# Graph layers on one core: the bias row laid by ScalarE under an adding load of x, a new order of the first graphs, and a chain per half of the last graph

## The chip, the cores and the metric

The kernel runs on one core of a Trainium2 chip. The metric is the device time of one execution in microseconds (us); lower is better. The engines are PE (TensorE), DVE (VectorE), ACT (ScalarE), POOL (GpSimd) and SP (SyncE, which here only issues DMAs). Sixteen DMA engines move data between HBM and SBUF.

## The reference, cut to what matters

There are 64 graphs of 256 nodes with 512 features. Each goes through two layers, all in fp32:

```
h  = relu(layernorm(x))
q, k, v = h @ Wq.T + bq, h @ Wk.T + bk, h @ Wv.T + bv
w  = adj * exp(q @ k.T);  w = w / sum(w, axis=2)
x1 = x + w @ v                                    # layer 0, with its residual
h1 = relu(layernorm(x1))
L  = (adj + I) scaled by d = (row sums)**-0.5 on both sides
y  = x1 + L @ (h1 @ W + b)                        # layer 1, with its residual
```

Since the rows of w sum to one, the value bias can be added behind the product: `x1 = (x + bv) + w @ (h @ Wv.T)`. The kernel keeps `x + bv` in the tile `xb`. The change is mostly about who makes `xb`.

## The kernel before

Everything is written by hand: each engine has its own program, which waits on semaphores. A product in fp32 is made of three fp32r products of rounded and rest parts (`_hi`, `_lo`), so each operand of TensorE is first split, as a rule by ACT (`_hi`) and DVE (`_lo`).

A function `steps` calls, on every engine, `step(0)`, `step(1)`, `step(2)`, a loop over 3 to 62, then `step(63)`, `step(64)` and `step(65)`. `step(k)` does the main part of graph k (flag `main`), the second layer of graph k-1 (`prev`) and the first preparations of graph k+1 (`ahead`). `step(0)` prepares weights and graph 1, `step(65)` is the second layer of the last graph alone.

On PE a steady step is, in this order: G (48 matmuls, `ps<-ht_hi,m_hi`, the weights Wq and Wk folded into m), the values V1 to V7 (42, `ps<-wt_hi,...`), Z of the graph before (24, `ps<-hat_hi,h_hi`: the normalized adjacency times h1), S (24, `ps<-ht_hi,g_hi`), O1 of the graph before (24 of 512 columns, `ps<-w_hi,z_hi`: the second layer's weight) and O (24, `ps<-v_hi,p_hi`).

`ht`, the transposed h, is made by a trip through HBM: ACT writes `h`, SP stores it (`h_scratch`), waits, loads it back in blocks of 32 by 32 with four DMAs of 128-byte rows (`h_blocks`), and DVE turns the blocks (L681, `transpose_h`). All this goes over SP's one queue. In SP's step the order is: `adj_in` (waits for `rsum_ready`, from ACT's `keep_adjacency`), the store of h, the four loads of `h_blocks`, the load of x into `xb` (L243), the load of x of two graphs on (`x_in`), the small trip of the row norms (`dn_scratch`, `dn_row`), the four `adj_blocks`, the two stores of y.

The steps that the change and the prediction touch:

- `xb`: SP loads x, POOL waits for it and adds `bv_row` (L345, two instructions a graph), after the power that makes `dn` (L334) and before its four sums `ht_sum` (L292 to L297). DVE reads `xb` when it makes x1 (L718, under the tile name `late`).
- DVE behind `h_blocks`: the two turns of `ht` (L681), `v_u`, `v`, `vk`, `v` (L642), `v<-v_u,v_p` (L644), `v_lo` (L648), `vk`, `v_lo` (L653), then `z_lo` (L785, twice), for which PE's O1 waits, then `v_lo` (L658), `p` (L798), and so on.
- The first graphs: ACT splits `w_hi` (L394) in `step(0)`; the layer norm of graph 2 is made in the middle of `step(1)`.
- The last graph: in `step(64)` PE does both halves of O1 of graph 63 and then O of graph 64; in `step(65)` DVE makes x1 and its statistics for both halves, POOL one power for both, ACT h1, DVE `h_lo`, then PE does Z and O1.

## Time and profile before

| | us |
|---|---|
| median of 3 runs | 1664.22 (1661.92 to 1664.26) |
| the profiled execution, its own time | 1666.89 |
| span of that execution, first to last instruction | 1665.1 |
| mean granted TensorE clock | 0.994 of full speed |
| PE busy | 1628.0 (98%) |
| DVE, ACT, POOL busy | 1434.1, 1071.2, 842.6 |

A row of the timeline reads: start, duration, engine, line, operation, output <- inputs, shape, count, and in brackets how long the engine had been idle before and who released it. Matmuls overlap, so the distance between two starts says what one costs. Engines with a q (SPq, ACTq) are queues of DMA issues: their duration is that of issuing, not of the transfer. All tiles that share the buffer `late` (wq, wk, x1, h1, x1b, y) are called `late`.

### The profile page before, as it was taken

The page shows a single profiled execution, that of the slowest core. Times are in us where ns is not written, and L with a number is a line of the kernel's source. Part 1 is how long each engine was busy: PE and PEld are TensorE (multiplying, and loading weights), DVE is VectorE, ACT ScalarE, POOL GpSimd, SP SyncE. Part 2 cuts the span into 40 slices and gives each one's busy share as a digit, 9 for nine tenths or more (in the row PEclk, how much of TensorE's full clock was granted, in tenths as well). Part 3 has the DMA queues.
Part 4 walks back from the last instruction along what each step waited for, and adds up shares of the span by engine and source line. Part 5 has one row for each costly group of instructions (what it writes and reads, how often), then busy time and mean ns, then how long its engine had stood idle before and what let it go on. Part 6 is the DMA issues. An engine that isn't in the chain of part 4 may idle for free.

```text
span 1665.1 us, 37788 instructions
## 1 busy us (share of the span) xinstructions
PE 1628.0 (98%) x12010; PEld 1544.7 (93%) x12010; DVE 1434.1 (86%) x3366; ACT 1071.2 (64%) x2451; POOL 842.6 (51%) x968
## 2 busy tenths in 40 slices
PE   8799999999999999999999999999999999999997
PEld 6789999999999999999999999999999999999996
DVE  6778888888889889888888888888888888888885
ACT  5656566676666666676576676676676676676552
POOL 2445555555555555555555555555555555555551
PEclk9999999999999999999999999999999999999999
DMA  5344544544544544544544544545544544544530
GB/s 171 89 127 119 145 121 125 148 121 119 153 120 120 152 120 122 152 124 124 145 125 123 148 121 119 152 122 125 148 122 122 149 126 126 143 123 122 147 98 29
DMA packets 494415, 212.66 MB, mean 128 GB/s; under 512 B 402496, under 2 KB 427072, under 8 KB 494400
## 3 DMA queue, kind: packets, MB, share of 16 engines
q1 hardware_dynamic: 492480, 210.89, 48.4%
q10 hardware_dynamic: 1920, 1.58, 0.3%
q8 instruction: 8, 0.13, 0.0%
q14 instruction: 7, 0.06, 0.0%
HBM read 146.28 MB, written 66.13 MB: 128 GB/s over the span
## 4 chain that ended last, share of the span: by engine, by line
PE 45%; DMA 14%; DVE 14%; ACT 10%; issue 9%; SPq 5%; POOL 3%; ACTq 0%; DVEq 0%; POOLq 0%
PE ps L854 15%; PE ps L856 14%; PE ps L857 14%; DMA h_blocks<-h_scratch 7%; DMA h_scratch<-h 6%; SPq L185 3%; ACT h L423 3%; DVE v L644 2%; ACT unused_x L436 2%; DVE z_lo L785 2%; DVE ht L681 1%; ACT adj_kept L445 1%; DVE v_lo L653 1%; ACT ht_hi L533 1%; ACT p_hi L524 1%
## 5 line engine op out<-in xcount | busy, mean ns | idle before, releaser
L345 POOL TENSOR_TENSOR xb<-xb,bv_row 128x512 f32<-128x512 f32 x128 | 169.0, 1341 | 432.7 <-DMA xb<-in_x_dram 394.3
L854 PE MATMUL ps<-ht_hi,m_hi 128*128 128x256 f32 x1024 | 286.2, 280 | 0.0
L856 PE MATMUL ps<-ht_lo,m_hi 128*128 128x256 f32 x1024 | 285.8, 279 | 0.0
L857 PE MATMUL ps<-ht_hi,m_lo 128*128 128x256 f32 x1024 | 285.6, 279 | 0.0
L413 ACT ACTIVATE g_hi<-ps,u_col 128x256 fp32r<-128x256 f32 x256 | 105.7, 464 | 204.9 <-PE ps L857 204.9
L854 PE MATMUL ps<-w_hi,z_hi 128*128 128x512 f32 x512 | 205.3, 401 | 11.9 <-DVE z_lo L785 11.8
L857 PE MATMUL ps<-w_hi,z_lo 128*128 128x512 f32 x512 | 203.0, 396 | 0.0
L856 PE MATMUL ps<-w_lo,z_hi 128*128 128x512 f32 x512 | 202.9, 396 | 0.0
L854 PEld LDWEIGHTS ps<-ht_hi,m_hi 128*128 128x128 f32 x1024 | 192.5, 188 | 0.0
L857 PEld LDWEIGHTS ps<-ht_hi,m_lo 128*128 128x128 f32 x1024 | 192.4, 188 | 0.0
L856 PEld LDWEIGHTS ps<-ht_lo,m_hi 128*128 128x128 f32 x1024 | 192.4, 188 | 0.0
L304 POOL TENSOR_TENSOR ht_sum_lo<-ht_sum,ht_sum_hi 128x512 fp32r<-128x512 f32 x128 | 163.5, 1299 | 13.5 <-ACT ht_sum_hi L408 11.4
L854 PE MATMUL ps<-hat_hi,h_hi 128*128 128x256 f32 x512 | 145.4, 284 | 7.7 <-DVE h_lo L747 7.7
L854 PE MATMUL ps<-wt_hi,ht_sum_hi 128*128 128x256 f32 (+1 forms) x512 | 144.9, 283 | 4.9 <-POOL ht_sum_lo L304 2.5
L854 PE MATMUL ps<-v_hi,p_hi 128*128 128x258 f32 (+1 forms) x512 | 144.6, 282 | 1.5 <-DVE ht_lo L822 0.9
L486 ACT ACTIVATE v_hi<-v 128x256 fp32r<-128x256 f32 x64 | 26.9, 421 | 184.1 <-DVE v L642 184.0
L857 PE MATMUL ps<-hat_hi,h_lo 128*128 128x256 f32 x512 | 145.2, 284 | 0.0
L856 PE MATMUL ps<-hat_lo,h_hi 128*128 128x256 f32 x512 | 145.1, 283 | 0.0
L857 PE MATMUL ps<-ht_hi,g_lo 128*128 128x256 f32 x512 | 145.1, 283 | 0.0
L856 PE MATMUL ps<-ht_lo,g_hi 128*128 128x256 f32 x512 | 144.6, 283 | 0.0
L854 PE MATMUL ps<-ht_hi,g_hi 128*128 128x256 f32 x512 | 144.6, 282 | 0.0
L856 PE MATMUL ps<-wt_lo,ht_sum_hi 128*128 128x256 f32 (+1 forms) x512 | 144.5, 282 | 0.0
(147 smaller groups left out, 5646.8 us busy)
## 6 DMA issues: line engine op xcount, KB each, us to landing
x_in<-in_x_dram SPq DMA_DIRECT2D x64, 512.0 KB, 5.0
xb<-in_x_dram SPq DMA_DIRECT2D x64, 512.0 KB, 4.4
out_dram<-late SPq DMA_DIRECT2D x128, 256.0 KB, 2.1
h_scratch<-h SPq DMA_DIRECT2D x62, 512.0 KB, 3.5
h_blocks<-h_scratch SPq DMA_DIRECT2D x248, 128.0 KB, 3.6
adj_in<-in_adj_dram SPq DMA_DIRECT2D x64, 256.0 KB, 2.9
adj_blocks<-in_adj_dram SPq DMA_DIRECT2D x256, 64.0 KB, 2.5
dn_row<-dn_scratch SPq DMA_DIRECT2D x64, 128.0 KB, 2.9
```

Of the source, the lines that this page charges most:

```text
L185: sp.dma_start(h_blocks[q * 32:(q + 1) * 32].rearrange("r c (g j) -> r c g j", j=32), rows[q]).then_inc(h_blocks_loaded, 16)
L304: pool.tensor_tensor(ht_sum_lo[:, pair], ht_sum[:, pair], ht_sum_hi[:, pair].bitcast(fp32), ALU.subtract).then_inc(ht_sum_lo_ready, 1)
L345: last = pool.tensor_tensor(xb[:, t, :], xb[:, t, :], bv_row[:], ALU.add)
L413: last = act.activation(g_hi[:, m, :], ps[:, G + j, m % 2 * N:m % 2 * N + N], ACT.Identity, bias=u_col[:, m:m + 1])
L423: act.activation(h[:, t, :], x_in[:, t, :], ACT.Relu, scale=rs_x[:, t:t + 1], bias=nb_x[:, t:t + 1]).then_inc(h_ready[t], 1)
L436: last = act.activation(unused_x[:, t, :], x_in[:, t, :], ACT.Square, bias=neg_mean[:, t:t + 1], accum_out=x_square[:, t:t + 1])
L486: act.activation(v_hi[:, 0, 1, 0:HD], v[:, 0, 1, 0:HD], ACT.Copy).then_inc(v_hi_ready[1], 1)
L644: dve.tensor_tensor(v[:, 1, 1, 0:HD], v_u3[:, 0:HD], v_p5[:], ALU.add).then_inc(v22_ready, 1)
L785: dve.tensor_tensor(z_lo[:, 2 * j:2 * j + 2, :].rearrange("p c n -> p (c n)"), ps[:, Z + j, :], z_hi[:, 2 * j:2 * j + 2, :].rearrange("p c ...
L854: pe.matmul(dst, a_hi[:, c, cols], b_hi[:, c, :], start=(first and c == 0), stop=False, skip_group_check=not first)
L856: pe.matmul(dst, a_hi[:, c, cols], b_lo[:, c, :], start=False, stop=False, skip_group_check=not first)
L857: end = pe.matmul(dst, a_lo[:, c, cols], b_hi[:, c, :], start=False, stop=(c == chunks - 1), skip_group_check=not first)
```

## The change

Three things are changed together.

1. `xb`: ACT copies `bv_row` into both halves of `xb` as soon as x1 of the graph before is made (`fill_xb`), and POOL issues a DMA that loads x and adds it to what lies in `xb` (`x_with_bias`, `accum_op=ADD`). SP's load of `xb` and POOL's two additions go.
2. The first graphs: `w_hi` is made on POOL; the adjacency of graph 1 is turned on DVE in `step(0)`; sums, squares and layer norm of graph 2 are made earlier; the transposed h of graph 2 has its own PSUM banks; `keep_p1` of step 2 comes between the halves of h1; 20 warm-up matmuls in place of 12. ACT now waits in `step(0)` for both bias rows ahead of its first sums.
3. The last graph: x1, statistics, power, scale and h1 go half by half; Z is made half by half; O1 of its second half goes in two pieces of 256 columns, each stored by itself; the second half of O1 of graph 63 comes behind O of graph 64.

In every step but the last, `v_lo` of L653 moves behind `z_lo`.

```diff
         def _(sp):
...
-            sp.dma_start(xb[:], x[0].rearrange("(t p) d -> p t d", p=P)).then_inc(xb_loaded, 16)
...
-                if main and prev:
-                    x_this = x_flat[bass.ds(sp.snap((this - 1) * (N * D)), N * D)]
-                    sp.wait_ge(x1_ready[0], this - 1)
-                    sp.wait_ge(x1_ready[1], this - 1)
-                    sp.dma_start(xb[:], x_this.rearrange("(t p d) -> p t d", p=P, d=D)).then_inc(xb_loaded, 16)
...
         def _(pool):
...
+            def x_with_bias(graph):
+                x_this = x_flat[bass.ds(pool.snap((graph - 1) * (N * D)), N * D)]
+                pool.wait_ge(xb_filled, graph)
+                pool.dma_start(xb[:], x_this.rearrange("(t p d) -> p t d", p=P, d=D),
+                               accum_op=ALU.add).then_inc(xb_ready, 16)
...
+                if main and prev:
+                    pool.wait_ge(d_ready, this - 1)
+                    pool.wait_ge(dn_turned_ready, this - 1)
+                    row_norms(this)
+                    x_with_bias(this)
                 if ahead and not main:
                     x_power(this + 1)
+                    row_norms(this + 1)
+                    x_with_bias(this + 1)
                     ht_sums(this + 1)
                     ht_sums_low(this + 1)
-                if main:
-                    if not prev:
-                        pool.wait_ge(bias_rows_loaded, 32)
-                    pool.wait_ge(xb_loaded, this * 16)
-                    for t in range(NT):
-                        last = pool.tensor_tensor(xb[:, t, :], xb[:, t, :], bv_row[:], ALU.add)
-                    last.then_inc(xb_ready, 1)
                 if main and not prev:
                     x_power(this + 1)
+                    pool.wait_ge(w_loaded, 16)
+                    pool.tensor_copy(w_hi[:], w_in[:]).then_inc(w_hi_ready, 1)
...
         def _(act):
...
+            def fill_xb():
+                for t in range(NT):
+                    last = act.activation(xb[:, t, :], bv_row[:], ACT.Copy)
+                last.then_inc(xb_filled, 1)
...
                     hat_high(this - 1)
+                if main and prev:
+                    act.wait_ge(x1_ready[0], this - 1)
+                    act.wait_ge(x1_ready[1], this - 1)
+                    fill_xb()
...
                 if ahead and not main:
+                    act.wait_ge(bias_rows_loaded, 32)
                     x_sums(this + 1)
                     x_squares(this + 1)
                     layer_norm_x(this, prev, older)
+                    fill_xb()
                     keep_adjacency(this + 1)
...
         def _(dve):
...
+                    transpose_adjacency(this + 1, False)
+                    turn_dn(this + 1, False)
                     for j in range(2):
                         dve.wait_ge(ht_done[j], this + 1)
...
         def _(pe):
...
-                for k in range(12):
+                for k in range(20):
...
+                if main and prev:
+                    first_result(0, this)
+                    if ahead:
+                        first_result(1, this)
...
+                if main and not ahead:
+                    first_result(1, this)
+                if prev and not main:
+                    last_graph(this - 1)
```

What POOL's program has in the loop, from the power that makes `dn` to its first sum of `ht`, before:

```order
L332 TENSOR_TENSOR rsum<-rsum,ones 128x2
L334 TENSOR_TENSOR dn_wide<-rsum,minus_half 128x2
L343 REGISTER_ALU
L345 TENSOR_TENSOR xb<-xb,bv_row 128x512 x2
L290 REGISTER_ALU
L292 TENSOR_TENSOR ht_sum<-ht 128x256
```

and of the change, with ACT's rows of the same stretch (from the sums of the adjacency to the scaling into h1) behind them:

```order
L288 TENSOR_TENSOR rsum<-rsum,ones 128x2
L290 TENSOR_TENSOR dn_wide<-rsum,minus_half 128x2
L295 ISA
L295 DMA xb<-in_x_dram 128x2x512
L301 REGISTER_ALU
L303 TENSOR_TENSOR ht_sum<-ht 128x256
```

```order
L450 ACTIVATE adj_kept,rsum<-adj_in 128x256 x2
L461 ACTIVATE hat_hi<-adjt 128x512
L456 ACTIVATE xb<-bv_row 128x512 x2
L418 ACTIVATE g_hi<-ps,u_col 128x256 x2
L488 ACTIVATE late<-late,nb,sc 128x512
```

The additions and their wait are gone from POOL; a DMA issue stands in their place, and ACT has two more copies between `hat_hi` and `g_hi`.

DVE's program at the start, from the shift of graph 1's layer norm to the first split of `ht`, before and then of the change:

```order
L672 TENSOR_TENSOR nb_x<-neg_mean,rs_x 128x2
L769 COPY ht<-ps 128x512 x2
L773 COPY wt<-ps 128x2x256 x2
L822 TENSOR_TENSOR ht_lo<-ps,ht_hi 128x512 x2
L570 TENSOR_TENSOR m_lo<-ps,m_hi 128x512 x4
```

```order
L697 TENSOR_TENSOR nb_x<-neg_mean,rs_x 128x2
L715 STREAM_TRANSPOSE adjt<-adj_blocks 128x512
L723 STREAM_TRANSPOSE dn_turned<-dn_wide 128x32
L848 COPY ht<-ps 128x512
L848 COPY ht<-ps 128x512
L852 COPY wt<-ps 128x2x256 x2
```

The turn of the adjacency blocks and the turn of `dn` now stand ahead of the copies of `ht`.

DVE's program for the last graph, from the last `p_lo` to the first rows of `h_lo`, before and then of the change:

```order
L842 SCALAR_TENSOR_TENSOR late<-ps,d,late 128x512 x2
L716 RECIPROCAL rinv<-ps 128x1
L718 SCALAR_TENSOR_TENSOR late<-ps,rinv,xb 128x512
L721 BN_STATS st<-late 128x6
L716 RECIPROCAL rinv<-ps 128x1
L718 SCALAR_TENSOR_TENSOR late<-ps,rinv,xb 128x512
L721 BN_STATS st<-late 128x6
L727 TENSOR_SCALAR d<-dn_wide 128x2
L729 BN_AGGR mv<-st 128x2 x2
L732 TENSOR_SCALAR ve<-mv 128x2
```

```order
L746 SCALAR_TENSOR_TENSOR late<-ps,d,late 128x512
L751 RECIPROCAL rinv<-ps 128x1
L753 SCALAR_TENSOR_TENSOR late<-ps,rinv,xb 128x512
L758 BN_STATS st<-late 128x6
L764 BN_AGGR mv<-st 128x2
L766 TENSOR_SCALAR ve<-mv 128x1
L751 RECIPROCAL rinv<-ps 128x1
L753 SCALAR_TENSOR_TENSOR late<-ps,rinv,xb 128x512
L770 TENSOR_TENSOR sc<-rs,dn_wide 128x1
L772 SCALAR_TENSOR_TENSOR nb<-mv,sc 128x1
```

The second y of graph 63 has moved behind these rows, and the scale of half 0 stands ahead of the statistics of half 1.

## Rows read from the trace of the kernel before

**Rows 1.** Waits of PE: who for whom, us in total, times, longest.

```profile
PE ps L854 <- DVE z_lo L785: 11.8, 15, 3.0
...
PE ps L854 <- ACT v_p L398: 3.2, 1, 3.2
...
PE ps L854 <- DVE v_u L627: 1.8, 1, 1.8
PE ps L889 <- ACT h L423: 1.7, 1, 1.7
```

**Rows 2.** Timeline: DVE's z_lo of one step, PE's first O1 of four steps.

```profile
75.20 1.27 DVE L785 TENSOR_TENSOR z_lo<-ps,z_hi 128x512 fp32r<-128x512 f32 x2
...
76.73 0.47 PE L854 MATMUL ps<-w_hi,z_hi 128*128 128x512 f32 x1 [0.60 <-DVE z_lo L785]
...
833.75 0.40 PE L854 MATMUL ps<-w_hi,z_hi 128*128 128x512 f32 x1
...
858.58 0.40 PE L854 MATMUL ps<-w_hi,z_hi 128*128 128x512 f32 x1
...
1633.57 0.40 PE L854 MATMUL ps<-w_hi,z_hi 128*128 128x512 f32 x1
```

**Rows 3.** Timeline of DVE in one step of the loop, from the turn of ht.

```profile
827.15 1.30 DVE L681 STREAM_TRANSPOSE ht<-h_blocks 128x512 f32<-128x512 f32 x2 [0.29 <-DMA h_blocks<-h_scratch]
...
829.67 1.46 DVE L644 TENSOR_TENSOR v<-v_u,v_p 128x256 f32<-128x256 f32 x1
...
831.51 0.50 DVE L653 TENSOR_TENSOR v_lo<-v,v_hi 128x256 fp32r<-128x256 f32 x1
831.94 1.27 DVE L785 TENSOR_TENSOR z_lo<-ps,z_hi 128x512 fp32r<-128x512 f32 x2
```

**Rows 4.** Timeline of POOL in the same step.

```profile
821.16 0.69 POOL L334 TENSOR_TENSOR dn_wide<-rsum,minus_half 128x2 f32<-128x2 f32 x1
828.30 2.55 POOL L345 TENSOR_TENSOR xb<-xb,bv_row 128x512 f32<-128x512 f32 x2 [6.46 <-DMA xb<-in_x_dram]
```

**Rows 5.** Timeline of the same step: DVE's second x1, ACT's first g_hi.

```profile
818.00 0.75 DVE L718 SCALAR_TENSOR_TENSOR late<-ps,rinv,xb 128x512 f32<-128x512 f32 x1
...
820.38 0.84 ACT L413 ACTIVATE g_hi<-ps,u_col 128x256 fp32r<-128x256 f32 x2 [3.20 <-PE ps L857]
```

**Rows 6.** Timeline of SP's issues in the same step.

```profile
821.05 2.84 SPq L185 DMA_DIRECT2D h_blocks<-h_scratch  x4
824.14 0.45 SPq L243 DMA_DIRECT2D xb<-in_x_dram  x1
```

**Rows 7.** DMA from 821 to 831 us: GB/s in 40 slices of 0.25 us.

```profile
GB/s 0 0 0 0 0 6 77 189 207 118 112 199 157 182 209 178 195 176 215 164 106 213 287 377 377 385 393 377 385 393 386 215 18 0 0 0 0 0 0 61
```

**Rows 8.** DMA from 6 to 13 us, by queue: q1 is SP's, q10 is ACT's.

```profile
q1 hardware_dynamic: 732, 1.42, 53.0%
q10 hardware_dynamic: 753, 1.38, 52.1%
```

**Rows 9.** Start: the bias row (issue, and landing below), ACT's sums, DVE.

```profile
4.79 0.53 ACTq L366 DMA_DIRECT2D b_row<-in_L_gnn_b_dram  x1
...
11.19 0.63 ACT L429 ACTIVATE unused_x<-x_in 128x512 f32<-128x512 f32 x1 [4.55 <-DMA x_in<-in_x_dram]
...
20.32 1.29 DVE L769 COPY ht<-ps 128x512 f32<-128x512 f32 x2 [3.62 <-PE ps L889]
...
31.51 6.51 DVE L608 TENSOR_TENSOR wt_lo<-wt,wt_hi 128x512 fp32r<-128x512 f32 x7
...
b_row<-in_L_gnn_b_dram ACTq DMA_DIRECT2D x1, 256.0 KB, 10.0
```

**Rows 10.** End: PE's first O of graph 64, then its first Z and O1.

```profile
1639.15 0.28 PE L854 MATMUL ps<-v_hi,p_hi 128*128 128x258 f32 x1
...
1649.84 0.55 PE L854 MATMUL ps<-hat_hi,h_hi 128*128 128x256 f32 x1 [7.66 <-DVE h_lo L747]
...
1656.03 0.47 PE L854 MATMUL ps<-w_hi,z_hi 128*128 128x512 f32 x1 [1.50 <-DVE z_lo L785]
```

More of the change, by code:

```diff
@@ L269, in _ @@
             steps(sp, step)
-            sp.wait_ge(stored, B * 16 * NT)
+            for a in range(2):
+                sp.wait_ge(y_ready[1], B + a)
+                sp.dma_start(out[B - 1, P:2 * P, a * HD:(a + 1) * HD], y[:, 1, a * HD:(a + 1) * HD]).then_inc(stored, 16)
+            sp.wait_ge(stored, B * 16 * NT + 16)
         @block.gpsimd
@@ L453, in step @@
             def step(this, prev, main, ahead, older=True, second=True):
+                if main and prev and not older:
+                    ht_sums_high(this)
                 if main and ahead and prev:
@@ L836, in step @@
-                if prev:
+                if main and ahead and prev:
+                    ht_low(this + 1, None)
+                if ahead and not main:
+                    ht_low(this + 1, HT[0])
+                    m_low()
+                    wt_sums()
+                    x_mean(this + 2)
+                    wt_low()
+                if main and not prev:
+                    w_low(slice(0, 2))
+                    x_mean(this + 2)
+                    w_low(slice(2, DC))
+                if prev and main:
@@ L925, in values @@
                     pe.wait_ge(y_ready[1], this - 2)
+                if prev and not older:
+                    pe.wait_ge(ht_ready[0], this)
+                    pe.wait_ge(ht_ready[1], this)
                 weights_ready(2)
```

274 lines of the change are left out of this document (170 added, 104 removed).

## The prediction, made before the changed kernel ran

> **What bounds the kernel now.** The engine shares come first: PE is busy 98% of the span (the table above), so nothing is won by making another engine's work shorter, unless PE waits for that work, and much can be lost if something becomes later. The views to read are therefore the waits of PE and, for each, the chain behind it.
>
> The waits of PE [rows 1] name three places. In the loop: O1 waits for DVE's `z_lo`, 11.8 us in 15 times. At the start: single waits of 1.7 to 3.2 us for `v_p`, `v_u` and `h` of the first graphs. The third is the last graph, whose waits come below. The loop's size: O1 starts at 833.75 and 858.58, a step of 24.83 us in which PE doesn't wait for `z_lo` [rows 2]. From 76.73 to 1633.57 us there are 62 steps, 1556.84 us, 25.11 each; the floor is 62 x 24.83 = 1539.5, so 17.4 us lie above it. About 7 of these lie in the first three steps, which still digest the start; the rest are steps in which `z_lo` came late.
>
> How near is the ordinary step to such a wait? On DVE [rows 3] the order from the turn of `ht` on is fixed: the turn begins at 827.15, after 0.29 us of waiting for `h_blocks`, and with nothing but queued work behind it `z_lo` ends at 831.94 + 1.27 = 833.21, and O1 starts at 833.75. Where PE is the one that waits, O1 follows the end of `z_lo` by 0.26 us (75.20 + 1.27 = 76.47, and 76.73) [rows 2]; here it follows by 0.54, so **the margin is about 0.3 us**. The trip of h through HBM that feeds the turn is also nearly as long as the step, since that 0.29 us of wait is there in a step of full speed. A delay of the landing by more than 0.3 us therefore lengthens the step one to one, in every step.
>
> The profiled execution took 1666.89 us (span 1665.1 and 1.8 around it), 2.67 above the median of 1664.22. I make the sums as differences to the profiled one and subtract them from 1664.
>
> **The change part by part. POOL's additions in the loop.** Two instructions, 2.55 us from 828.30 [rows 4], go. They lie over DVE's L644, which adds two SBUF tiles and takes 1.46 us there [rows 3], against 0.50 us for L653 of the same shape. So their going gives DVE 0 to 1.0 us ahead of `z_lo`; as POOL's four `ht_sum` come next on its queue and may run earlier, over other rows of DVE, I take 0.7. Moving L653 behind `z_lo` gives 0.4 more (831.94 - 831.51) [rows 3]; it is then ahead of the next split of v, which PE needs only for O, after O1's 24 matmuls, and costs nothing there. With both the margin is 0.3 + 0.7 + 0.4 = **1.4 us**. What of the 10 us of stalls in the loop is due to landings less than 1.1 us late goes: I take 3 us, since the longest wait of 3.0 [rows 1] isn't covered by 1.1, and the first steps start late for other reasons.
>
> **ACT's copies.** Two of 128x512, each as ACT's sums of x, 0.63 us (its row comes with the start), 1.2 us in all. They are queued behind x1's second half, which ends at 818.75, and ahead of `g_hi`, before which ACT idled 3.20 us, to 820.38 [rows 5]. They end at about 818.75 + 0.1 + 1.2 = 820.05: hidden, with 0.3 us to spare. If that cover were gone, `g_hi` would be late, then S; S stands behind Z on PE, so some us lie between, and I cost it at nothing.
>
> **The adding load.** POOL issues it after the power, at 821.16 + 0.69 = 821.85 at the earliest [rows 4]. POOL idled 6.46 us before its additions, so its own time for the issue is covered, up to 6 us. Before, x for `xb` was queued on SP at 824.14, behind the four `h_blocks`, which were issued from 821.05 to 823.9 [rows 6]. Now it has its own queue and can move while `h_blocks` moves. This is the term that decides. The DMA's rate [rows 7] shows the blocks from 822.3 to 826.3 us at 110 to 215 GB/s, and then xb and the next `x_in` at 377 to 393: 512 KB take 1.35 us of all engines. If the load falls among the blocks, it takes time from them. That two queues share evenly is seen at the start, where q1 moved 1.42 MB in 732 packets while q10 moved 1.38 in 753 [rows 8]. Since the packets of x are 2 KB and those of h 128 bytes, equal turns let all of x through within the blocks' transfer. The bounds of the blocks' delay: 0 (x comes behind, or uses time that the blocks, at half the full rate, leave empty); 1.35 (it displaces them for its whole length); and 2.7 (an adding packet costs double, since it must fetch `xb` too; the trace shows no adding load, so this is 2 x 1.35). Below 1.4 it disappears in the margin. I take 0.7, the middle of the first two, because the blocks leave half the rate unused: cost **nothing**. At 2.7 the step grows by 1.3 us.
>
> The Trainium skill speaks against my reading: "DMA: Bandwidth & Descriptors", in its section on queues and completion order, says that a DMA engine takes turns between its queues packet by packet. By that rule x isn't behind the blocks but among them; the counts of the two queues at the start agree for plain packets, and what an adding packet costs no row here shows. By the rule the delay would be at least the 1.35 of a plain load, which still fits the margin of 1.4, and my forecast would stand on its edge. "SBUF — State Buffer" adds, in its part on the port that DVE and GpSimd share, that some DVE operations keep GpSimd from writing the descriptors of its DMAs; by it the load would move later, towards the place behind the blocks, which would help here.
>
> **The start.** ACT now waits for both bias rows before its sums. `b_row` is issued at 4.79 and lands 10.0 later, at 14.8, where the sums started at 11.19 [rows 9]: 3.6 later; the sums were followed by about 1 us of waiting for DVE, which goes, so h is 2.6 later. The fill, 1.2 us, lies ahead of the sums of the adjacency, and DVE's copies of `ht` now stand behind `turn_dn`, which needs POOL's power of those sums: the copies move from 20.32 [rows 9] to about 24.4, by 4.1. Between them and G of graph 1 stand only splits on ACT and DVE, with just under 1 us of idle time; G moves by 3.2. Given back: the seven splits `wt_lo`, which ran beside POOL's additions, took 6.51 us [rows 9], and at 0.69 each (an unshared split of this shape: 1.27 for two with one start, so 0.6 to 0.7) they take 4.8, 1.7 less. Then come the waits for `v_u` 1.8, `h` 1.7 and 1.3 of the 3.2 for `v_p` [rows 1], 4.8 together: the turn of the adjacency and `g_lo` no longer stand ahead of `v_u`, graph 2's layer norm is made earlier, and `keep_p1` comes ahead of the second half of h1. 3.2 - 1.7 - 4.8 = -3.3; I take **-3**, with -6 (the first steps' 7 us shrink too) and +3 (all of G's delay stays) as ends.
>
> **The end.** O of graph 64 comes ahead of the last 12 of O1(63)'s 24 matmuls, which ran from 1633.57 [rows 2] to 1639.15 [rows 10]: 2.8 us, of which I count 2.4, since O1's first half has to cover `p_lo`; the 12 then fill a part of the gap. Half by half, DVE's chain to `h_lo` has half the work ahead of the first power. Z started at 1649.84 after 7.66 us idle [rows 10]; I put its start at 1646.3 (2.4 from the order, and 1.1 from the halves, about two of DVE's passes of 0.7). From there Z and O1 are the same work, with the wait of 1.50 between them gone: 3.5 + 1.5 = **5 us** gained, between 3 (only the order helps) and 6.
>
> **Sum:** start -3, loop -3, end -5: -11, and 1664 - 11 = **1653**.
>
> **The rivals.**
> *Slower: the adding load displaces the blocks (chance 0.24).* Place: `h_blocks` from 822 to 826. It decides when the delay passes 1.4 us. For it: issue at 821.85 against 821.05 for the first block [rows 4, 6], large against small packets, an addition that must read its target. Against it: the blocks leave half the rate free. Start and end stay at -8. Delay 1.7: 61 steps x 0.3 = 18, and 1664 - 8 + 18 = 1674; delay 2.7: 61 x 1.3 = 79, and 1664 - 8 + 79 = 1735.
> *The start doesn't pay (0.10).* All four waits come back elsewhere and G's delay stays: +3, loop 0, end -5: 1662, within the noise.
> *The load lands clear of the blocks and the larger margin takes all late landings (0.08).* Then SP's queue is shorter too, `x_in` starts at 824.14 instead of behind xb; 10 us of stalls go: -3 -10 -5 = 1646.
> *Mine (0.58),* own range 1645 to 1662.
>
> **How the numbers follow.** A measurement of this kernel can tell about 0.2%, 3.3 us, from no change. The forecast and the fourth case are faster, and so nearly all of their 0.66, less 0.02 for the upper edge of mine: 0.64. The third is the same: 0.10. The slower one, with 0.02 added for unforeseen waits, is 0.26. The range: the fastest case reaches 1643 to 1647, and the slow one spreads from 1674 to 1735; to leave out no more than 2 in 10 I go from 1643 to 1700, which cuts the worst half of the slow case.
>
> **What would show it.** On SP no issue of `xb`; on POOL one at about 822, landing by 826 to 827. DVE's turn of `ht` starting with less than 1.4 us of wait and L644 at 0.5 to 0.8 us; O1 every 24.83 us without waits for `z_lo`. At the start ACT's sums at 14.8 and G of graph 1 some 3 us later; at the end the last Z some 3.5 us sooner against O1(63). I am wrong if DVE waits longer for `h_blocks` than 1.4 us in each step (then the step grows by the excess), if the landing of xb comes after its reader x1 needs it, or if the wait for the bias rows is followed through the first three steps.

## The result, and the profile after

The changed kernel takes **1785.68 us** (median of 4 runs, 1779.71 to 1787.98) against 1663.26 of the kernel before: a ratio of **1.073**, 95% interval 1.071 to 1.075. It is 7.3% slower. The profiled execution, the fastest of the four, took 1779.71, with a span of 1778.0.

The page: the line of the engines, and two lines of the DMA queues (packets, MB, share of the time of 16 engines; q1 is SP's queue, q0 GpSimd's).

```profile
PE 1656.0 (93%) x12038; PEld 1562.3 (88%) x12038; DVE 1347.1 (76%) x3370; ACT 1123.5 (63%) x2578; POOL 721.4 (41%) x906
...
q1 hardware_dynamic: 475216, 177.33, 40.9%
q0 software_dynamic: 17408, 33.56, 11.7%
```

The waits (who for whom, us in total, times, longest), which answer to [rows 1].

```profile
DVE ht L706 <- DMA h_blocks<-h_scratch: 225.6, 62, 4.8
...
PE ps L933 <- DVE z_lo L862: 105.2, 62, 2.9
```

PE waited for `z_lo` in 15 steps before; now it waits in all 62, and in each DVE has first waited for the blocks of h. One step of the loop, from the timelines of SP, POOL, DVE and PE, answers to [rows 2 to 4] and [rows 6].

```profile
846.61 2.79 SPq L186 DMA_DIRECT2D h_blocks<-h_scratch  x4
...
846.65 0.69 POOL L290 TENSOR_TENSOR dn_wide<-rsum,minus_half 128x2 f32<-128x2 f32 x1
847.29 1.25 POOL L295 DMA_DIRECT2D xb<-in_x_dram  x1
...
856.29 1.30 DVE L706 STREAM_TRANSPOSE ht<-h_blocks 128x512 f32<-128x512 f32 x2 [3.94 <-DMA h_blocks<-h_scratch]
...
858.81 0.66 DVE L667 TENSOR_TENSOR v<-v_u,v_p 128x256 f32<-128x256 f32 x1
...
861.41 0.47 PE L933 MATMUL ps<-w_hi,z_hi 128*128 128x512 f32 x1 [2.00 <-DVE z_lo L862]
```

Two spans tell the story. From the issue of the first block to the turn of `ht`: 827.15 - 821.05 = 6.10 us before [rows 3, 6], 856.29 - 846.61 = **9.68** now. From the turn to O1: 833.75 - 827.15 = 6.60 before, with PE not waiting [rows 2, 3], 861.41 - 856.29 = **5.12** now. Over the loop's steps the medians of the first are 6.23 before and 9.56 after: the blocks land 3.3 us later. The second, in the steps in which PE waits, is 6.30 before and 5.12 after: DVE's part is 1.18 shorter.

The transfer's speed in the same step, 846 to 858 us in 40 slices of 0.3 us, which answers to [rows 7]:

```profile
GB/s 27 0 0 0 0 0 18 101 211 125 140 158 105 31 35 153 212 207 209 184 201 217 204 183 194 213 240 217 177 199 218 246 322 335 172 22 0 0 0 0
```

The rate alone hides what happens. Counted from the records of single packets of that step, by the us in which they began (128 bytes are the blocks, 2048 bytes of q0 the adding load; ns is the mean time of one):

```
from us   blocks, 128 B   adding load, 2 KB
848       1064 (13 ns)    -
849        856 (13 ns)     8 (767 ns)
850        120 (13 ns)    43 (195 ns)
851         32 (27 ns)    96 (186 ns)
852        138 (22 ns)    92 (176 ns)
853       1288 (13 ns)    17 (176 ns)
854        598 (15 ns)    -
```

From 850 to 853 the blocks nearly stand still: 290 packets in 3 us, where they make over 1000 in one. Over the whole execution an adding packet took 202 ns in the mean (median 176), a plain packet of 2 KB 84 in the median. The 256 adding packets of a graph, at 202 ns, make 3.23 us of all 16 engines, close to the 3.33 by which the turn is late. The landings of the four block loads say the same (medians over the loop, counted from the first issue): the first two land after 3.12 and 4.01 us, as before (3.12 and 4.13), the last two after 8.28 and 9.36 in place of 5.13 and 6.04.

**Where the 112.9 us of span went.** Before, the first O1 began at 76.73, 62 steps took 1556.8 and the rest from O1 of graph 63 took 31.5 [rows 2]. After, from PE's timeline:

```profile
77.03 0.47 PE L933 MATMUL ps<-w_hi,z_hi 128*128 128x512 f32 x1 [2.25 <-DVE z_lo L862]
```

The 62 steps from there took 1674.2, to 1751.24, and the rest 26.8. So the start is 0.3 later, the loop 117.4 longer (27.00 a step), the end 4.7 shorter. The medians are 122.4 apart: the profiled execution of the changed kernel lies 6.0 below its median and that of the kernel before 3.6 above its own, and where those 9.6 us lie no trace shows.

Not all of the 117.4 is the delay itself. In the loop of the changed kernel TensorE's granted clock stood at the lower of its two levels (1.2 in place of 2.4 GHz) for 37.5 us in all, within ten of the 62 steps; in the loop before it was 6.8 us. Two neighbouring steps: the stretch, its length, the busy time of PE, its weight loads, DVE, ACT and POOL, then the mean granted clock (1.00, then 0.94 of full speed), DMA share and GB/s:

```profile
1397.00:1423.82 26.82, 25.07 (x186) 23.83 (x187) 20.67 (x54) 17.37 (x41) 11.19 (x14) 1.00 0.55 123
1423.82:1452.50 28.68, 26.64 (x186) 24.98 (x187) 20.73 (x54) 17.38 (x41) 11.18 (x14) 0.94 0.51 116
```

The ten steps take 28.30 us in the mean, the other 52 take 26.75. That is 1.92 over the floor of 24.83, and 62 x 1.92 - 17.4 = 102 us of the loop's loss are the delay; 10 x 1.55 = 15.5 us are the clock. In the second step shown PE is busy 1.57 us longer for the same 186 matmuls. Those ten steps begin with waits of PE for `z_lo` of 1.76 to 2.82 us; over the others the mean wait is 1.61. In e1, e3, h1 and h2 below, whose mean waits are under 0.9 us, the granted clock never fell in the loop.

### The profile page after: what moved, and what is told of

It reads as the page before. It is cut to its first block, busy times and chain, and to the rows that moved or that the text cites. A ratio compares the mean times of both kernels' runs of the same rounds, so it can differ in the third digit from the quotient of the medians.

```text
span 1778.0 us, 37794 instructions
## 1 busy us (share of the span) xinstructions
PE 1656.0 (93%) x12038; PEld 1562.3 (88%) x12038; DVE 1347.1 (76%) x3370; ACT 1123.5 (63%) x2578; POOL 721.4 (41%) x906
## 4 chain that ended last, share of the span: by engine, by line
DMA 38%; ACT 22%; issue 13%; SPq 9%; DVE 9%; PE 7%; ACTq 1%; DVEq 0%; POOL 0%; POOLq 0%
DMA h_blocks<-h_scratch 25%; DMA h_scratch<-h 12%; SPq L186 7%; ACT unused_x L434 4%; ACT h L428 3%; ACT unused_x L441 3%; ACT adj_kept L450 3%; DVE ht L706 3%; ACT e L538 2%; PE ps L933 2%; PE ps L935 2%; PE ps L936 2%; ACT ht_hi L548 2%; ACT p_hi L544 2%; SPq L227 2%
## 5 line engine op out<-in xcount | busy, mean ns | idle before, releaser
L933 PE MATMUL ps<-w_hi,z_hi 128*128 128x512 f32 (+1 forms) x516 | 214.7, 416 | 105.3 <-DVE z_lo L862 105.2
L303 POOL TENSOR_TENSOR ht_sum<-ht 128x256 f32<-128x256 f32 x64 | 46.7, 729 | 559.0 <-DVE ht L706 551.9
L706 DVE STREAM_TRANSPOSE ht<-h_blocks 128x512 f32<-128x512 f32 x124 | 81.0, 691 | 225.6 <-DMA h_blocks<-h_scratch 225.6
L933 PEld LDWEIGHTS ps<-w_hi,z_hi 128*128 128x128 f32 x516 | 101.0, 196 | 137.9 <-issue 116.3
L935 PE MATMUL ps<-w_lo,z_hi 128*128 128x512 f32 (+1 forms) x516 | 209.2, 406 | 0.0
L936 PE MATMUL ps<-w_hi,z_lo 128*128 128x512 f32 (+1 forms) x516 | 209.1, 405 | 0.0
L456 ACT ACTIVATE xb<-bv_row 128x512 f32<-128x512 f32 x128 | 73.8, 625 | 130.2 <-DVE late L753 130.2
L935 PE MATMUL ps<-v_lo,p_hi 128*128 128x258 f32 (+1 forms) x512 | 144.9, 283 | 0.0
L936 PE MATMUL ps<-wt_hi,ht_sum_lo 128*128 128x256 f32 (+1 forms) x512 | 144.7, 283 | 0.0
```

Of the source, the lines that this page charges most:

```text
L303: pool.tensor_tensor(ht_sum[:, S1], a21, a22, ALU.add).then_inc(ht_sum_ready, 1)
L456: last = act.activation(xb[:, t, :], bv_row[:], ACT.Copy)
L706: dve.transpose(ht[:, 2 * j:2 * j + 2, :].rearrange("p c n -> p (c n)"), h_blocks[:, 2 * j:2 * j + 2, :].rearrange("p c n -> p (c n)")).th ...
L933: pe.matmul(dst, a_hi[:, c, cols], b_hi[:, c, :], start=(first and c == 0), stop=False, skip_group_check=not first)
L935: pe.matmul(dst, a_hi[:, c, cols], b_lo[:, c, :], start=False, stop=False, skip_group_check=not first)
L936: end = pe.matmul(dst, a_lo[:, c, cols], b_hi[:, c, :], start=False, stop=(c == chunks - 1), skip_group_check=not first)
```

## The experiments

All times below are medians of runs, beside runs of the kernel before on the same chip: 1661.59 us beside the e kernels, 1662.5 beside f, 1662.68 beside g and 1665.6 beside h. "First O1" is its start in the profiled execution, "step" the mean of 62 steps from it, "end" what follows the start of O1 of graph 63, "turn" the median from the issue of the blocks to the turn of `ht`. From the timelines:

```
kernel             us        first O1   step    end    turn
before             1663.26    76.73     25.11   31.5   6.23
changed            1785.68    77.03     27.00   26.8   9.56
e1_plain_load      1705.32    74.84     25.88   26.7   8.70
e2_add_late        1644.96    78.62     24.83   26.2   6.23
e3_half_add        1677.94    76.51     25.34   27.0   8.17
e4_old_xb          1659.55    73.11     25.11   24.9   6.29
f1_late_and_start  1641.00    72.60     24.84   26.2   6.25
f2_late_l653_back  1643.07    78.52     24.84   26.5   6.23
f3_xb_alone_late   1648.68    78.26     24.83   32.3   6.24
f4_small_add       1643.26    76.09     24.84   26.9   6.62
g1_no_additions    1649.96    75.73     24.84   32.3   6.39
g2_xb_alone_early  1812.32    81.34     27.44   32.3   9.58
g3_plain_on_act    1647.19    78.09     24.85   26.9   7.22
g4_additions_late  1671.09    77.83     25.12   32.3   6.30
h1_plain_act_mid   1691.87    74.96     25.57   25.8   8.38
h2_plain_2kb       1695.71    78.97     25.64   25.0   8.41
```

### Is it the adding load among the blocks?

**e1_plain_load.** POOL's load of x becomes a plain one.

```diff
-                pool.dma_start(xb[:], x_this.rearrange("(t p d) -> p t d", p=P, d=D),
-                               accum_op=ALU.add).then_inc(xb_ready, 16)
+                pool.dma_start(xb[:], x_this.rearrange("(t p d) -> p t d", p=P, d=D)).then_inc(xb_ready, 16)
```

> The changed kernel with POOL's load of x made a plain load: same queue, same place, same bytes, ACT's copies kept; the value bias is left out of x1. Theory (the price is that of the adding packets, which take twice and more the time of plain ones and hold the blocks of h back by 3.6 us against a margin of 1.4): plain packets of 88 ns hold the blocks back by about 1.35, which the margin takes: O1 every 24.9 us, 1652 to 1662 us. Rival 1 (a second queue beside the blocks is enough, whatever its packets do): 26 us or more a step, over 1730. Rival 2 (ACT's two copies delay the step): 27.0 as before the edit, about 1785.

Measured: 1705.32 us, ratio 1.0256 (1.0226 to 1.0286), 25.88 us a step. Neither: over the floor of 24.83 the plain load costs 1.05 us a step where the adding one costs 2.17, about half, and far from nothing. My theory was right that the adding packets are dearer, and wrong that a plain load fits into the margin: the turn comes 8.70 us after the issue, 2.5 later than before, where I had bounded a plain load at 1.35. ACT's copies as the cause fall: they are all here, and most of the loss is gone.

**e2_add_late.** The adding load is issued behind the four sums of `ht`, when the blocks have landed.

```diff
                     row_norms(this)
-                    x_with_bias(this)
+                    if not ahead:
+                        x_with_bias(this)
...
                     ht_sums(this + 1)
+                    if prev:
+                        x_with_bias(this)
```

> The changed kernel with POOL's adding load issued behind the four sums of ht, when the blocks of h have landed, instead of ahead of them. Nothing is left out. Theory (overlap with the blocks is the cause): no wait beyond the margin, O1 every 24.8 to 24.9 us, 1648 to 1658 us. Rival 1 (second queue) says the same, unless the load now holds back the adjacency blocks, the row norms or its own reader x1: then 25.5 or more, over 1700. Rival 2 (ACT's copies): 27.0, about 1785.

Measured: **1644.96 us**, ratio 0.989 (0.986 to 0.992): 1.1% faster than the kernel before and some 141 us faster than the changed one, for one DMA issue that stands four instructions lower. One step in the timelines of SP, POOL, DVE and PE:

```profile
810.58 2.86 SPq L186 DMA_DIRECT2D h_blocks<-h_scratch  x4
...
816.91 1.30 DVE L709 STREAM_TRANSPOSE ht<-h_blocks 128x512 f32<-128x512 f32 x2 [0.20 <-DMA h_blocks<-h_scratch]
...
821.76 1.27 POOL L295 DMA_DIRECT2D xb<-in_x_dram  x1 [0.26 <-issue]
...
823.61 0.40 PE L936 MATMUL ps<-w_hi,z_hi 128*128 128x512 f32 x1
```

The turn waits 0.20 us, and O1 has no bracket: it waits for nothing. From turn to O1 it is 6.70, against 5.12 in the steps in which PE waits: the margin is now some 1.6 us.

**e3_half_add.** Half of the adding load.

```diff
-                pool.dma_start(xb[:], x_this.rearrange("(t p d) -> p t d", p=P, d=D),
+                pool.dma_start(xb[:, 0:1, :], x_this.rearrange("(t p d) -> p t d", p=P, d=D)[:, 0:1, :],
                                accum_op=ALU.add).then_inc(xb_ready, 16)
```

> The changed kernel with only the first 128 rows of x loaded and added (256 KB in place of 512); x is left out of the second half of x1. Theory: half of the adding packets hold the blocks back by about 1.8 us, 0.4 over the margin of 1.4: O1 every 25.2 us, 1665 to 1685 us. Rival 1 (second queue, a fixed price): well over 1700. Rival 2 (ACT's copies): 1785.

Measured: 1677.94 us, 25.34 a step, the turn 1.94 later than before: as the theory says. PE waits for `z_lo` in 34 of the 62 steps.

**f4_small_add.** An eighth of the bytes, in 128 packets of 512 bytes.

```diff
-                pool.dma_start(xb[:], x_this.rearrange("(t p d) -> p t d", p=P, d=D),
+                pool.dma_start(xb[:, 0:1, 0:128], x_this.rearrange("(t p d) -> p t d", p=P, d=D)[:, 0:1, 0:128],
                                accum_op=ALU.add).then_inc(xb_ready, 16)
```

> The changed kernel (early adding load) with 128 of 1024 columns' worth of x in its load: 128 packets of 512 bytes, 64 KB; the rest of x is left out of x1. Theory (the blocks wait for the time that the adding packets take): packets of 45 to 180 ns, so 0.4 to 1.4 us of delay, within the margin: O1 every 24.83 to 24.95 us, 1643 to 1653 us. Rival (an adding load beside the blocks costs a fixed wait of its own, in the queue or in writing its descriptors): over 25.2 a step, over 1665.

Measured: 1643.26 us, 24.84 a step, the turn 0.39 later. Its packets took 67 ns in the mean. So an adding load in the same place, on the same queue, is free when it is short; the rival of a fixed price falls.

These kernels make a line. With the time of q0's packets a graph (the sum over the execution, by 16 engines and 64 graphs), against the delay of the turn and the step:

```
                 packets of x, us   turn later by, us   step, us
e2_add_late      3.27 (elsewhere)   0.00                24.83
f4_small_add     0.54               0.39                24.84
e3_half_add      1.58               1.94                25.34
changed          3.23               3.33                27.00
```

The step grows only where the delay passes about 1.4 us (1.94 - 0.51 = 1.43), which is the margin of the prediction. From the changed kernel it would be 3.33 - 2.17 = 1.16, but that step contains the clock; its 52 steps at full clock give 3.33 - 1.92 = 1.41.

### Where in the change does the rest lie?

**e4_old_xb.** The changed kernel with `xb` made as before; only the first graphs, the last graph and L653's place are changed.

```diff
+                if main and prev:
+                    x_this = x_flat[bass.ds(sp.snap((this - 1) * (N * D)), N * D)]
+                    sp.wait_ge(x1_ready[0], this - 1)
+                    sp.wait_ge(x1_ready[1], this - 1)
+                    sp.dma_start(xb[:], x_this.rearrange("(t p d) -> p t d", p=P, d=D)).then_inc(xb_filled, 16)
                 if second and prev:
                     load_x(this)
...
-                pool.dma_start(xb[:], x_this.rearrange("(t p d) -> p t d", p=P, d=D),
-                               accum_op=ALU.add).then_inc(xb_ready, 16)
+                for t in range(NT):
+                    last = pool.tensor_tensor(xb[:, t, :], xb[:, t, :], bv_row[:], ALU.add)
+                last.then_inc(xb_ready, 16)
...
-                    fill_xb()
...
-                    act.wait_ge(bias_rows_loaded, 32)
```

> The changed kernel with xb made as before (SP's load behind the blocks, POOL's two additions, no copies on ACT), so that only the first graphs, the last graph and L653's new place are changed. All theories: the loop returns to about 25.0 us a step, the end keeps the 4.8 us that the changed kernel shows, the start 0 to -3: 1652 to 1660 us. If the first graphs themselves cost time, 1662 or more.

Measured: 1659.55 us against 1661.59, ratio 0.9992 (0.9976 to 1.0009), so no difference that these runs can tell. In its profiled execution (1656.63 us) the parts are plain: first O1 at 73.11, 3.6 earlier, and the end 24.9, 6.6 shorter; the loop is 25.11 a step as before. Two things follow. L653's place shows no gain in the loop while POOL's additions are there, although turn to O1 in a waiting step fell from 6.30 to 5.86. And the gains at both ends, 10 us in the profiled pair (spans 1654.8 and 1665.1), show as 2 in the medians; single runs of both kernels lie up to 9 us apart, and I can't split the medians further.

**f1_late_and_start.** On top of e2, ACT no longer waits for the bias rows ahead of its first sums.

```diff
-                    act.wait_ge(bias_rows_loaded, 32)
                     x_sums(this + 1)
                     x_squares(this + 1)
                     layer_norm_x(this, prev, older)
-                    fill_xb()
...
                     wt_high()
+                    act.wait_ge(bias_rows_loaded, 32)
+                    fill_xb()
...
-                    x_with_bias(this + 1)
                     ht_sums(this + 1)
                     ht_sums_low(this + 1)
+                    x_with_bias(this + 1)
```

> The kernel with the late adding load (1645 us), and in the first step ACT no longer waits for the bias rows ahead of its sums: it waits for them and fills xb of graph 1 behind the splits of the values' weights, and POOL issues its adding load behind the sums of graph 1. Theory (the bias rows and the fill hold back the first graph: the kernel with the old way of making xb had its first O1 at 73.1, the late one at 78.6): first O1 at 73 to 74.5, loop 24.83, 1639 to 1642 us. Rival (the first O1 depends on the blocks of h of graph 3 and not on this wait): 1644 to 1646.

Measured: **1641.00 us**, ratio 0.987 (0.984 to 0.989), the first O1 at 72.60 instead of 78.62. The first O1 is 6.0 us earlier in this pair of executions; the medians are 4.0 below e2 and 2.1 below f2, which has the wait and the fill too, so they cost some 2 to 4 us. This is the lowest median found, 1.3% below the kernel before, but the interval of f2 (0.9845 to 0.9906) overlaps its own. The first sums of ACT, in the changed kernel and then here:

```profile
15.21 0.63 ACT L434 ACTIVATE unused_x<-x_in 128x512 f32<-128x512 f32 x1 [2.07 <-DMA b_row<-in_L_gnn_b_dram]
```

```profile
11.38 0.63 ACT L437 ACTIVATE unused_x<-x_in 128x512 f32<-128x512 f32 x1 [4.65 <-DMA x_in<-in_x_dram]
```

**f2_late_l653_back.** On top of e2, the split goes back ahead of `z_lo`.

```diff
                     value_low(this)
+                    value_low_upper(this)
                 if prev:
...
-                    value_low_upper(this)
                     value_low_lower(this)
```

> The kernel with the late adding load, and the split of L653 back ahead of z_lo. Theory (with POOL's additions gone and the blocks undisturbed the margin is 1.6 us, of which the split takes 0.4): no measurable change, 1643 to 1647 us, O1 every 24.83 to 24.85 us. Rival (the split's place is what brought the loop to its floor): 25.0 or more a step, over 1653.

Measured: 1643.07 us, 24.84 a step: nothing. The move is free, and not needed.

**f3_xb_alone_late.** The kernel before, with nothing but the new `xb`, its load late.

```diff
-                    sp.dma_start(xb[:], x_this.rearrange("(t p d) -> p t d", p=P, d=D)).then_inc(xb_loaded, 16)
...
                     hat_high(this - 1)
+                if main and prev:
+                    act.wait_ge(x1_ready[0], this - 1)
+                    act.wait_ge(x1_ready[1], this - 1)
+                    fill_xb()
...
-                    for t in range(NT):
-                        last = pool.tensor_tensor(xb[:, t, :], xb[:, t, :], bv_row[:], ALU.add)
...
                     ht_sums(this + 1)
+                    if prev:
+                        x_with_bias(this)
```

> The kernel before, with xb alone changed: ACT fills it with the bias row, POOL's adding load comes behind the four sums of ht. First and last graphs, and L653's place, as before. Theory (taking POOL's additions away and the load out of SP's queue ends the stalls of the loop, 10 us and more): O1 every 24.83 to 24.9 us, first O1 at 76.7, last O1 of graph 63 to the end 31.5 us: 1647 to 1653 us. Rival (the loop's gain in the late kernel comes from L653 or the first graphs): 1658 to 1662.

Measured: 1648.68 us, ratio 0.991 (0.989 to 0.994), 24.83 a step. The idea of part 1, in a place that suits it, takes away the stalls of the loop but for one of 1.5 us.

**g1_no_additions.** The kernel before without POOL's additions, SP's load of `xb` kept.

```diff
-                    pool.wait_ge(xb_loaded, this * 16)
-                    for t in range(NT):
-                        last = pool.tensor_tensor(xb[:, t, :], xb[:, t, :], bv_row[:], ALU.add)
-                    last.then_inc(xb_ready, 1)
+                    if not prev:
+                        pool.wait_ge(xb_loaded, this * 16)
+                        for t in range(NT):
+                            last = pool.tensor_tensor(xb[:, t, :], xb[:, t, :], bv_row[:], ALU.add)
+                        last.then_inc(xb_ready, 1)
```

> The kernel before with SP's plain load of xb where it was, and POOL's two additions left out from graph 2 on, so the value bias is left out of x1 there. Nothing else is changed. Theory (the additions, which hold back the chain behind the turn of ht, make the loop's stalls): O1 every 24.83 to 24.9 us, 1646 to 1653 us. Rival (the 512 KB in SP's queue, which delay the next load of x, make them): 25.0 or more a step, 1657 or more.

Measured: 1649.96 us, 24.84 a step, 2 waits of PE for `z_lo` in place of 15. It was the additions, not the 512 KB in SP's queue.

**g4_additions_late.** The kernel before with the additions behind the sums of `ht`.

```diff
-                    pool.wait_ge(xb_loaded, this * 16)
-                    for t in range(NT):
-                        last = pool.tensor_tensor(xb[:, t, :], xb[:, t, :], bv_row[:], ALU.add)
-                    last.then_inc(xb_ready, 1)
...
                     ht_sums(this + 1)
+                    if prev:
+                        add_value_bias(this)
```

> The kernel before with POOL's two additions moved behind its four sums of ht; nothing is left out and nothing else changed. Theory (they hurt through L644 ahead of z_lo): the sums are 2.6 us earlier and may themselves hold back rows ahead of z_lo, so a part comes back: O1 every 24.85 to 25.0 us, 1648 to 1658 us. Rival (the additions' place doesn't matter, only SP's load of xb does): 25.1, 1660 to 1664.

Measured: 1671.09 us against 1662.68, ratio 1.0052 (1.0035 to 1.0069): half a per cent slower, outside both forecasts, though the step of 25.12 us in its profiled execution is the rival's 25.1 and that of the kernel before. So the trace shows that the gain of the missing additions is gone, and not where the median's 8 us lie. In its timeline of POOL and DVE:

```profile
829.21 2.99 POOL L286 TENSOR_TENSOR xb<-xb,bv_row 128x512 f32<-128x512 f32 x2
...
829.76 1.28 DVE L663 TENSOR_TENSOR v_lo<-v,v_hi 128x512 fp32r<-128x512 f32 x1
830.96 1.52 DVE L803 TENSOR_TENSOR p<-e,adjt 128x256 f32<-128x256 f32 x1
```

L644, with its line number now L649, is quick again (0.65 us in this step), but the additions now lie over a split that takes 1.28 us (0.69 in e2) and over `p`, which takes 1.52 (0.42 in e2). The work behind `z_lo`, which I had not counted, stands ahead of x1 of the same step on DVE's queue; that it is this delay which comes back as late blocks is my reading, not shown. Additions of two SBUF tiles on POOL held DVE up in both places.

**g2_xb_alone_early.** f3 with the load at the changed kernel's place.

```diff
                 if main and prev:
+                    x_with_bias(this)
...
                     ht_sums(this + 1)
-                    if prev:
-                        x_with_bias(this)
```

> The kernel before with the new way of making xb alone, POOL's adding load at the changed kernel's place ahead of the sums of ht; first and last graphs and L653's place as before. Theory: the landing of the blocks is 3.3 us late as in the changed kernel, and the margin lacks the 0.4 us of L653: O1 every 27.4 us, 27.2 to 27.6; 62 x 27.4 + 76.7 + 31.5 = 1807 and 2 around it, 1795 to 1822 us. Rival (L653's place is worth nothing here either): 27.0, about 1785.

Measured: 1812.32 us, ratio 1.088 (1.085 to 1.092), 27.44 a step. Part 1 alone makes the whole loss. The difference to the changed kernel, 27.44 - 27.00, isn't all L653's place: the clock fell in 17 of these steps and in ten of the changed kernel's. At full clock it is 27.00 (45 steps) against 26.75, so 0.25 us a step; from turn to O1, where L653 stood, it is 5.51 against 5.12.

### Why a plain load costs as much as it does

**g3_plain_on_act.** A plain load of x on ACT's queue, behind the fill.

```diff
                     fill_xb()
+                    act.wait_ge(xb_filled, this)
+                    x_this = x_flat[bass.ds(act.snap((this - 1) * (N * D)), N * D)]
+                    act.dma_start(xb[:], x_this.rearrange("(t p d) -> p t d", p=P, d=D)).then_inc(xb_plain, 16)
```

> The changed kernel with a plain load of x issued by ACT right behind its fill of xb, on ACT's hardware queue, in place of POOL's adding load; the value bias is left out of x1. Theory (any second queue takes turns with the blocks by the packet): like POOL's plain load, the blocks land 2 to 2.7 us late, O1 every 25.5 to 26.0 us, 1685 to 1712 us. Rival (only GpSimd's queue does this): landing under 1.4 us late, O1 every 24.9 us, 1645 to 1655.

Measured: 1647.19 us, 24.85 a step, the turn 0.99 later. It reads like the rival, but it isn't a test of it: ACT issued the load at 810.32 and the blocks were issued at 811.03, so by the packet records x had passed before most blocks began to move. The run misses its question; what it shows is that a load that goes ahead of the blocks, at 84 ns a packet, costs under 1 us.

**h1_plain_act_mid.** The same load, issued behind the first half of h1.

```diff
-                    act.wait_ge(xb_filled, this)
-                    act.dma_start(xb[:], x_this.rearrange("(t p d) -> p t d", p=P, d=D)).then_inc(xb_plain, 16)
...
+                        if main and t == 0:
+                            act.wait_ge(xb_filled, this)
+                            act.dma_start(xb[:], x_this.rearrange("(t p d) -> p t d", p=P, d=D)).then_inc(xb_plain, 16)
```

> As the kernel with ACT's plain load, but issued behind the first half of h1, so that its packets meet the blocks of h in the middle of their transfer; the value bias is left out of x1. Theory (any second queue takes turns packet by packet, so x goes through at once while the blocks nearly stand): turn of ht 1.4 to 2.6 us later against its issue than without such a load (7.6 to 8.8 us instead of 6.23), O1 every 24.9 to 26.0 us, 1650 to 1712 us, and in the trace the blocks' packets drop to one per packet of x. Rival (only GpSimd's queue goes ahead): the turn 7.2 us after the issue or less and the blocks' packets keep their rate.

Measured: 1691.87 us, ratio 1.017 (1.0147 to 1.0193), 25.57 a step, the turn 8.38 us after the issue. From its timelines of ACT and DVE:

```profile
805.76 0.38 ACTq L496 DMA_DIRECT2D xb<-in_x_dram  x1
...
813.54 1.31 DVE L711 STREAM_TRANSPOSE ht<-h_blocks 128x512 f32<-128x512 f32 x2 [2.48 <-DMA h_blocks<-h_scratch]
```

So it isn't GpSimd's queue: a plain load on ACT's queue among the blocks does the same. In the 2 us from 807 the blocks got 217 and 245 packets for 56 and 165 of x; the step is within the theory's range, the packets are more than its one for one. The delay adds up here. x's packets are 1.48 us a graph, and the blocks' own packets got dearer: all packets of 128 bytes took 5.63 us a graph against 4.97 before (14.9 ns each in the mean against 13.2; in the 2 us behind x, 22). 1.48 + 0.66 = 2.14, and the turn is 8.38 - 6.23 = 2.15 late.

**h2_plain_2kb.** e1 with a DMA for each half, meant to make its packets 2 KB.

```diff
-                pool.dma_start(xb[:], x_this.rearrange("(t p d) -> p t d", p=P, d=D)).then_inc(xb_ready, 16)
+                rows = x_this.rearrange("(t p d) -> p t d", p=P, d=D)
+                for t in range(NT):
+                    pool.dma_start(xb[:, t, :], rows[:, t, :]).then_inc(xb_ready, 16)
```

> As the kernel with POOL's plain load, but as two DMAs of one half each, so that its packets are 2 KB and not 4 KB; the value bias is left out of x1. Theory (the delay is the time of x's packets plus what they cost the blocks beside them; size plays no part): turn of ht 8.5 to 8.9 us after the issue, O1 every 25.8 to 26.0 us, 1700 to 1712 us. Rival (the 4 KB packets are what holds the blocks back beyond 1.4 us): 7.6 to 8.0 us, O1 every 24.9 to 25.2 us, 1650 to 1665 us.

Measured: 1695.71 us, 25.64 a step, the turn 2.18 late, 8.41 us after the issue: a little under the theory's ranges and far over the rival's. But the packet records show 8192 packets of 4 KB, as in e1, so the size didn't change and this run can't decide between the two; the question of size stays open on GpSimd's queue. h1's packets are of 2 KB and cost the same, which speaks against the rival.

## Why the prediction was wrong, point by point

**The bound, its chain and the margin: right.** The prediction put the margin after the change at 1.4 us and said that beyond it every us of delay lengthens the step. The half load gives 1.43, the changed kernel's steps at full clock 1.41, and DVE's part of the chain is 1.18 shorter where the prediction summed 1.1 (0.7 from the additions, 0.4 from L653). L644 takes 0.66 us where 0.5 to 0.8 was forecast.

**The step that failed: "I take 0.7, the middle of the first two, because the blocks leave half the rate unused: cost nothing."** The delay is 3.3 us, 1.9 beyond the margin in each step, where 0.7 was to vanish in it. Three things were wrong in it. First, the reason: the unused half of the rate in [rows 7] isn't free capacity. The blocks keep the engines busy with small packets; the line that stands above [rows 7] in the same view of the kernel before, which I did not use, shows it:

```profile
DMA  0000004997699999999999899999999600000001
```

Each digit is the busy share of a slice of 0.25 us from 821 on, in tenths; the blocks run from the first 4 on, at 9 in nearly every slice. With that row the argument against the rival was gone. Second, the plain load: bounded at 1.35, measured 2.15 (h1) to 2.5 (e1); in part this is because the blocks' own packets took longer beside it (0.66 us a graph in h1, 0.6 in e1). Third, the adding packets: taken as at most 2 x 1.35 = 2.7, measured 3.2 (202 ns a packet in the mean, median 176 against 84), so even the upper bound was too low.

**The rule of the Trainium skill.** "DMA: Bandwidth & Descriptors", in its section on queues and completion order, had said that an engine takes turns between its queues packet by packet. The page means by a packet a bundle, typically of 9 to 17 descriptors, and the trace agrees with that better than with turns of one for one. The 256 packets of x in the profile's count are 16 for each engine. At each instant looked at (every 0.2 us from 851.1 to 852.7) 16 to 19 packets of x were under way and 0 to 3 of the blocks, and in the us from 851 the blocks got 32 packets for 96 of x. That is what one sees if each engine works off its 16 packets of x in one turn while the blocks stand, 16 x 0.2 = 3.2 us; the records don't name the engines, so it is a reading. I weighed the rule and then priced its outcome at 1.35, under the margin.

**The rival that came true** is the slower one, to which 0.24 was given, with 1674 to 1735 us. Its place and its threshold are what was measured; its price was too low, 79 us for the loop where 117 came, of which the clock, which no rival had, made 15.5. 62 x (27.00 - 24.83) = 134.5 us over the floor, less the 17.4 that were there before, is that 117; -3 and -5 at the ends came out as +0.3 and -4.7.

**The start: the gain of 3 didn't come.** The changed kernel has +0.3. Without the wait and the fill the sum would have given -1.7 - 4.8 = -6.5; e4, which has neither, shows -3.6 (73.11). The wait and the fill were taken at +3.2; f1 shows 2 to 4 in the medians and 6.0 in the first O1 of one pair. More can't be read from single executions: nine kernels with this same start have their first O1 between 74.84 and 78.97, and four with the old start (before, f3, g1, g4) between 75.73 and 78.26.

**The end: right.** 31.5 became 26.8, with -5 forecast, and the wait of 1.50 ahead of the last O1 is gone. The first Z of the last graph waits 3.44 us in place of 7.66 [rows 10], from PE's timeline of the changed kernel:

```profile
1763.81 0.55 PE L1047 MATMUL ps<-hat_hi,h_hi 128*128 128x256 f32 x1 [3.44 <-DVE h_lo L731]
```

**ACT's copies: right.** The two take 1.15 us (a mean of 0.625 for one) and end 0.38 us before `g_hi` is due:

```profile
844.34 1.15 ACT L456 ACTIVATE xb<-bv_row 128x512 f32<-128x512 f32 x2 [1.77 <-DVE late L753]
845.87 0.84 ACT L418 ACTIVATE g_hi<-ps,u_col 128x256 fp32r<-128x256 f32 x2 [0.38 <-PE ps L936]
```

**What stays open.** Why packets of 128 bytes take up to twice their time behind a plain load on another queue; e1's delay of 2.5, of which 1.46 are x's packets and 0.6 dearer blocks, leaves 0.4 without a name, while in h2 the same sum (1.81 and 0.49) is 0.1 over the delay of 2.18. SP's issue of the four blocks took 4.9 us in the median in h1 and 3.6 in e1, against 2.8 before. The four issues begin as before, and in h1 already the first load lands 2.3 us later, so the issue isn't what holds that one back, but what it does to the last one wasn't tested. Why turn to O1, shorter by 0.4 in e4, didn't shorten its mean step was not settled.

## What to carry to other kernels

A transfer moved to another engine's queue is no longer behind what it was queued behind: before moving it, look at the busy share of the DMA engines (not their GB/s) while the critical transfer runs, and issue the moved one where that share is low, by standing it behind an instruction that waits for the critical one. A stream of small packets was the weak side of such a meeting here: about the time of all the other queue's packets was added to it. Work taken off an engine by an adding DMA is a good trade when the DMA has its own time slot: here the same change is worth -1.1% in one place of POOL's program (e2) and +7.3% four instructions higher.

## What the runs showed of the hardware

- An adding packet of 2 KB into SBUF took 176 ns in the median (202 in the mean), a plain one 84; an adding packet of 512 bytes 67 in the mean. A plain packet of 4 KB on GpSimd's queue took 159 in the median.
- Beside another queue's packets of 2 or 4 KB, a queue with packets of 128 bytes fell from over 1000 packets in a us to between 32 and 138 (adding load), to 104 in the lowest us of the step at 812.86 in e1 (plain, 4 KB) and to 217 and 245 in h1 (plain, 2 KB). Being issued first didn't save it: the blocks were issued first in all three.
- In the loop of the changed kernel, with waits of TensorE of 1.7 us a step in the mean, the granted clock stood at the lower level for 37.5 us, and not once in the loops of e1, e3, h1 and h2 (waits under 0.9 us in the mean). From O1 to the next issue of the blocks, a step with such a stretch took 13.57 us against 12.11.
- An issue of a DMA by POOL kept POOL for 1.25 us, one by ACT took 0.38 (POOL's was an adding load; the plain one of e1 took 0.78).
- Two additions of SBUF tiles on POOL slowed DVE's operations with two SBUF inputs in each place where they were put: 1.46 us for L644 in the kernel before, 1.28 for a split of 128x512 and 1.52 for `p` in g4, against 0.65, 0.69 and 0.42 in e2.
